# Post-norm block of low-rank attention and a top-2 mixture of experts: shorter score stacks, earlier loads of x, and an expert stage that begins while the last batches' tail is still open

## The chip, the cores and the metric

One core of one Trainium2 chip runs the whole program in one launch. The metric is device time in microseconds (us), the median of several executions. The engines are named as in the profile: PE is TensorE (matmuls), DVE is VectorE, ACT is ScalarE, POOL is GpSimd and SP is SyncE, which here only waits and issues DMAs.

## The reference

The input x is 16 batches of 512 tokens of 128 channels. Cut to what matters:

```python
q, k, v = heads(x @ Wq.T + bq), heads(x @ Wk.T + bk), heads(x @ Wv.T + bv)      # 16 heads of 8
zq, zk, zv = q @ V, k @ V, v @ V                                                # V, U: 8 x 8
att = softmax(einsum('bhqr,bhkr->bhqk', zq, zk) / sqrt(8))
y = einsum('bhqk,bhkr->bhqr', att, zv) @ U.T
x = layernorm(x + merge(y) @ Wo.T + bo)
p, i = top_k(softmax(x @ gate_w.T), 2); p = p / sum(p)
h = relu(einsum('td,ehd->teh', x, w1) + b1)                                     # 8 experts, 512 hidden
out = einsum('ted,te->td', einsum('teh,edh->ted', h, w2) + b2, combine(p, i))
return layernorm(x + out)
```

Only the two chosen experts of a token count, so the kernel routes each of the 8192 tokens to two experts instead of computing all eight.

## The kernel before

There are three stages, one behind the other, with a barrier between them.

**Setup** (L227 to L367). The weights are folded, and SP fills rows of the score stacks in device memory that never change: 16 stores of blank rows and rows of ones (`blank`, `k_ones`, L241 to L248), whose landing SP waits for (`blanks_stored`) ahead of a store of blank token rows (`routed_d<-pad_rows`, L252), which it waits for too. The first attention work can't begin before this block has ended on every engine.

**Attention** (L408 to L968). The function `schedule` (L408) unrolls bodies n = -2 to 17 with 32 steps each. The body of batch n holds its own scores, and besides: the projections of batch n+2 (transposition of x, L457; q and k, L465 and L488), v of batch n+1, the row maxima of the next scores, which run 24 steps ahead (LAG), and what follows the attention of n-1 and n-2: normalisation, output projection (L480), layernorm, gate (L526), choice of the two experts, ranks (L494, L497), and the scatter of token rows to their experts' areas in device memory (`routed_d`, POOL, L855, 8 indirect DMAs per batch). So the bodies of n = 16 and 17 hold no scores, only that tail.

- q and k are each split in three bf16 parts. The products of parts are made by one matmul: a *stack* of rows holds them one below the other, 8 positions of 8 ranks, 64 rows, for each of two heads. Six positions are pairs of parts, one (`MAX_POS`) holds the three parts of the row maximum against rows of ones, one is blank. Maxima (`maxima`, matmul in L583; DVE reduces them, L808) and scores (`scores`, matmul in L565; ACT takes the exponential, L694) both run over all 64 rows.
- SP stores the parts of a batch (L920), waits for them, and loads the stacks by head group (L925, per group one DMA of 256 KB for k and one for q), then the first half of the max rows (L913, 6 small DMAs), then the third group; in the next body the fourth. x of batch n+2 (L930) is loaded at the start of body n. All of this is one in-order queue.
- PE's order of work is written out by hand: at step s the score matmuls of s, the maxima of s+24, every other step the four products with v (`av`, L546), and `misc(s)`, a piece of other work.

**Experts** (L1018 to L1240). 136 tiles of 128 routed tokens. Per tile: SP reads the tile's row from a table and loads 128 rows (L1039), PE transposes (L1057), multiplies with W1 (L1066) and, two tiles later, with W2 (L1074); ACT copies the expert's weights three tiles ahead (L1109) and applies the relu (L1117); DVE copies the transposition out (L1140 to L1142), adds biases (L1163, L1147) and combines (L1151); POOL halves x (L1200) and scatters the result rows (L1205). The table (DVE, `table` steps, L820 to L838) is made when the last batch has been routed. `loop_tiles` (L1018) unrolls 8 tiles, loops, and unrolls the last 8. The final layernorm over 16 batches follows (L1101, L1178 to L1227).

## Time and profile before

| | us |
|---|---|
| median of 3 runs | 1254.78 (1251.57 to 1260.56) |
| the profiled execution | 1257.83 |
| its span, first to last recorded instruction | 1255.7 |
| PE busy | 1064.8 (85% of the span) |
| DVE busy | 972.6 (77%) |
| ACT busy | 904.7 (72%) |
| POOL busy | 588.2 (47%) |

The profile is of one execution: each instruction with start and duration. "Busy" is the time in which an engine executed anything. A duration in a row that says x6 covers six instructions. What stands in square brackets behind a row is how long the engine had been idle and what released it. PEclk is the share of TensorE's full clock that was granted.

### The profile page before, as it was taken

Reading aid. Unit: us, or ns where it says so; the run is one execution under the profiler, and the core shown is the slowest. Engines: PE = TensorE matmul, PEld = TensorE weight load, DVE = VectorE, ACT = ScalarE, POOL = GpSimd, SP = SyncE. Lnnn points to the kernel's source line nnn. Section 1 sums busy time; section 2 is a strip of 40 time slices with the busy share of each in tenths; the row PEclk is TensorE's granted clock in tenths of the full one; section 3 lists DMA queues with packets and bytes.
Section 4 is the critical chain, followed back from the end, with each engine's and each line's share of the span. In section 5 each row is a group of like instructions: output and inputs, shape, how many; then the busy total and the mean of one; then the engine's idle time right before and its main releaser. Section 6 shows DMA issues by size and latency. Waiting matters only on the chain. (4 is left out here: it accounts for less than half of the span.)

```text
span 1255.7 us, 24651 instructions
## 1 busy us (share of the span) xinstructions
PE 1064.8 (85%) x7711; PEld 515.8 (41%) x7711; DVE 972.6 (77%) x2115; ACT 904.7 (72%) x1177; POOL 588.2 (47%) x827
## 2 busy tenths in 40 slices
PE   3378899889898888999989899888728999999967
PEld 2132222222222222222222222222218999999952
DVE  2378889789888898887988779698246888888845
ACT  1047788677787777867778677687718999999937
POOL 1123145272452634527245171521354777777745
PEclk9989999899999999988999889899958999999989
DMA  2932241332523315233252332410012222222246
GB/s 68 282 117 58 80 135 43 111 102 59 148 56 99 108 52 148 65 90 103 57 148 57 97 103 56 121 34 15 18 49 64 70 68 69 69 69 70 67 154 263
DMA packets 108789, 114.31 MB, mean 91 GB/s; under 512 B 19816, under 2 KB 82066, under 8 KB 108704
## 3 DMA queue, kind: packets, MB, share of 16 engines
q1 hardware_dynamic: 99104, 92.10, 25.8%
q0 software_dynamic: 8448, 16.93, 4.3%
q10 hardware_dynamic: 1152, 4.19, 0.8%
q8 instruction: 47, 0.77, 0.3%
q14 instruction: 38, 0.31, 0.1%
HBM read 64.45 MB, written 48.44 MB: 90 GB/s over the span
## 5 line engine op out<-in xcount | busy, mean ns | idle before, releaser
L808 DVE TENSOR_REDUCE row_max<-score_ps 128x2 f32<-128x1024 f32 x512 | 617.9, 1220 | 134.6 <-PE score_ps L583 94.0
L694 ACT ACTIVATE probs<-score_ps 128x1024 f32<-128x1024 f32 x512 | 521.7, 1023 | 150.8 <-PE score_ps L565 130.3
L546 PE MATMUL av_ps<-probs,v_one 128*9 128x512 f32 x2048 | 277.8, 615 | 8.2 <-ACT probs L694 6.4
L583 PE MATMUL score_ps<-k_stack,q_stack 64*128 64x512 bf16 x1024 | 204.0, 396 | 74.6 <-ACT probs L694 55.6
L565 PE MATMUL score_ps<-q_stack,k_stack 64*128 64x512 bf16 x1024 | 204.0, 396 | 24.2 <-DVE row_max L808 19.0
L389 POOL TENSOR_TENSOR max_parts<-neg_max,zeros 32x128 bf16<-32x128 f32 x32 | 14.3, 446 | 386.9 <-ACT neg_max L635 386.9
L1109 ACT ACTIVATE w_cur<-experts 128x1156 f32 x136 | 158.5, 1167 | 36.5 <-PEq L425 17.2
L565 PEld LDWEIGHTS score_ps<-q_stack,k_stack 64*128 64x128 bf16 x1024 | 49.2, 93 | 315.1 <-issue 156.6
L1205 POOL DMA_INDIRECT y_d<-y_out,place x136 | 136.8, 1006 | 43.4 <-issue 43.4
L855 POOL DMA_INDIRECT routed_d<-rows,slot_i x128 | 125.4, 980 | 62.2 <-issue 36.6
L1066 PE MATMUL up_ps<-xt_sb,w_cur 128*128 128x128 f32 x1088 | 145.6, 277 | 0.0
L1074 PE MATMUL down_ps<-w_cur,hidden_r 128*128 128x128 f32 x1088 | 143.4, 275 | 0.0
L1066 PEld LDWEIGHTS up_ps<-xt_sb,w_cur 128*128 128x128 f32 x1088 | 134.1, 194 | 0.0
L1074 PEld LDWEIGHTS down_ps<-w_cur,hidden_r 128*128 128x128 f32 x1088 | 132.3, 192 | 0.0
L583 PEld LDWEIGHTS score_ps<-k_stack,q_stack 64*128 64x128 bf16 x1024 | 51.5, 95 | 131.6 <-ACT probs L694 87.8
L1163 DVE TENSOR_TENSOR hidden<-up_ps,w_cur 128x512 f32<-128x512 f32 x136 | 93.7, 689 | 3.6 <-PE up_ps L1066 3.2
L1117 ACT ACTIVATE hidden_r<-hidden 128x512 f32<-128x512 f32 x136 | 85.2, 626 | 6.7 <-DVE hidden L1163 5.2
L1200 POOL TENSOR_TENSOR half_x<-x_rows_sb,halves 128x128 f32<-128x128 f32 x136 | 53.4, 393 | 35.8 <-DVE y_out L1151 26.2
L546 PEld LDWEIGHTS av_ps<-probs,v_one 128*9 128x9 f32 x2048 | 30.6, 88 | 89.9 <-issue 84.5
L1147 DVE TENSOR_TENSOR y_bias<-down_ps,w_cur 128x128 f32<-128x128 f32 x136 | 39.6, 291 | 28.9 <-issue 26.0
L623 ACT ACTIVATE y_sb<-av_ps 128x512 f32<-128x512 f32 x64 | 38.2, 598 | 29.0 <-remote 16.6
L1057 PE MATMUL xt_ps<-ident,x_rows_sb 128*128 128x128 f32 x136 | 37.8, 278 | 18.0 <-DMA x_rows_sb<-routed_d 18.0
(189 smaller groups left out, 1144.5 us busy)
## 6 DMA issues: line engine op xcount, KB each, us to landing
k_stack<-k_stack_d SPq DMA_DIRECT2D x64, 256.0 KB, 3.6
q_stack<-q_stack_d SPq DMA_DIRECT2D x64, 256.0 KB, 4.2
x_rows_sb<-routed_d SPq DMA_DIRECT2D x136, 65.0 KB
q_stack_d<-q_parts SPq DMA_DIRECT2D x32, 192.0 KB
...
```

Source lines behind the costliest of these rows:

```text
L546: last = nc.tensor.matmul(av_ps[32 * g:32 * g + V_COLS, :], v_one[n.parity][:, kb, HG * hg + g, :], probs[:, (2 * j + g // 2) % P_RING, g ...
L565: last = nc.tensor.matmul(exp_bank(b, s)[:, a, :], k_stack[b.parity][at, c, kb * P:(kb + 1) * P], q_stack[b.parity][at, c, :], start=True, ...
L583: last = nc.tensor.matmul(max_bank(b, s)[:, a, :], q_stack[n.parity][at, c, g * P:(g + 1) * P], k_stack[n.parity][at, c, :], start=True, s ...
L694: nc.scalar.activation(probs[:, s % P_RING, :, :], exp_bank(b, s)[:, :, :], ACT.Exp).then_inc(S["exp_done"], 1)
L808: nc.vector.tensor_reduce(row_max[:, m // (STEPS // 2), :, m % (STEPS // 2)], max_bank(b, s)[:, :, :], AX.X, ALU.max).then_inc(S["red_done ...
L855: nc.gpsimd.indirect_dma_start(routed_d, bass.IndirectOffsetOnAxis(ap=slot_i[n.parity][:, w, t:t + 1], axis=0), rows[n.parity][:, w, t, :] ...
L1066: last = nc.tensor.matmul(up_ps[u % 4][:, h * P:(h + 1) * P], w_cur[u][:, h * P:(h + 1) * P], xt_sb[u % 2][:, :], start=True, stop=True)
L1074: last = nc.tensor.matmul(down_ps[u % 2][:, :], hidden_r[u % 4][:, h, :], w_cur[u][:, HID + h * D:HID + (h + 1) * D], start=(h == 0), stop ...
L1109: nc.scalar.activation(w_cur[u][:, :], experts[:, bass.ds(e, 1), :].rearrange("p a h -> p (a h)"), ACT.Copy).then_inc(M["w_copied"], 1)
L1117: nc.scalar.activation(hidden_r[u % 4][:, :, :], hidden[u % 4][:, :, :], ACT.Relu).then_inc(M["relu_out"], 1)
L1163: nc.vector.tensor_tensor(hidden[u % 4][:, :, :], up_ps[u % 4][:, :].rearrange("p (h t) -> p h t", t=P), w_cur[u][:, B1].unsqueeze(2).to_b ...
L1205: nc.gpsimd.indirect_dma_start(y_d, bass.IndirectOffsetOnAxis(ap=place[u][:, :], axis=0), y_out[u][:, :], None, bounds_check=2 * B * T - 1 ...
```

## The change

Three things are done.

1. The stacks get 6 positions of 8 ranks: maxima run over 48 rows, scores over 51, the three last being the parts of the row maximum. The rows of ones in k's stack are set once in SBUF, by two DVE memsets of 128 x 4096 bf16 at the start. The 16 stores of blank rows go, with the wait for them; the blank token rows are still stored, not waited for in setup. A stack is loaded by two DMAs of 96 KB instead of one of 256 KB, one for each half of the partitions. The k parts of the first batch are stored from ACT's queue.
2. x is loaded one body sooner: in the body of n SP loads batch n+3 (as soon as x of n+1 has been transposed), where it loaded n+2.
3. `schedule` ends with the body of batch 15. The experts begin with 32 full tiles (`FIRST`) filled by tokens of batches 0 to 13, by a table of their own (`first_tiles`, 18 small DVE operations in the body of batch 15). Their rows are loaded by SP, 12 tiles ahead of the block's end, 20 behind it, into a buffer of 32 tiles. The tail of batches 14 and 15 is cut into pieces, and `attention(j)` writes the pieces behind (on PE: ahead of) the work of tile j on each engine. At tile 31 SP stores the pads, waits for the table of the rest and for all scatters, and loads tile 32. All tiles use one PSUM buffer for the transposition, where there were two.

```diff
-POS = 8
-MAX_POS = 5
-MAX_ROW = MAX_POS * R
-ROWS = POS * R
+POS = 6
+ROWS = 64
+SCORE_ROWS = POS * R
+MAX_ROWS = 3
...
+FIRST = 32
+FIRST_GROUP = 4
+FIRST_EARLY = 12
...
-                    sp.wait_ge(bo_loaded, 16)
-                    sp.wait_ge(blanks_ready, 4)
-                    for n in range(2):
-                        for stack_d, row, tile in ((q_stack_d[n], MAX_POS, blank), (q_stack_d[n], POS - 1, blank),
-                                                   (k_stack_d[n], MAX_POS, k_ones), (k_stack_d[n], POS - 1, blank)):
-                            for a in range(2):
-                                sp.dma_start(stack_d[a, row, :, :, :].rearrange("r c t -> (r c) t"),
-                                             tile[a * ROWS:(a + 1) * ROWS, :]).then_inc(blanks_stored, 16)
-                    sp.wait_ge(blanks_stored, 16 * 16)
...
-                    sp.wait_ge(pads_stored, 16)
...
+                    for n in range(2):
+                        nc.vector.memset(k_stack[n][:, :, :], 1.0).then_inc(ones_ready, 1)
...
-                for n in range(-2, B + 2):
+                for n in range(-2, B):
...
-                                at = slice(a * ROWS, (a + 1) * ROWS)
+                                at = slice(a * ROWS, a * ROWS + SCORE_ROWS + MAX_ROWS)
...
-                        if proj and not is_first(b) and not is_first(p1):
...
+                            n3 = n1 + 2
...
+                            sp.dma_start(x_in[n3.parity][:, :, :], tokens(x_rows, n3)).then_inc(x_loaded[n3.parity], 16)
...
+                        if proj and not is_first(b):
...
+                            if t < FIRST - 1:
+                                return
+                            for loaded in first_loaded:
+                                sp.wait_ge(loaded, 16 * FIRST_GROUP)
+                            store_pads()
+                            sp.wait_ge(rest_table, REST_STEPS)
+                            sp.wait_ge(pads_stored, 16 + 16 * E)
+                            for n in range(2):
+                                sp.wait_ge(scattered[n], B // 2 * 8 * 16)
+                            return
...
+                        if j == 0:
+                            pe.wait_ge(S["yn_sb"], n15.count(HG, 3))
+                            y_transpose(pe, n15, 3)
+                        elif j == 1:
+                            pe.wait_ge(S["yn_sb"], n15.count(HG, 4))
+                            y_to_rows(pe, n15)
+                        elif j == 2:
+                            pe.wait_ge(S["ynt_sb"], n15.count(1, 1))
+                            project_out(pe, n15)
+                        elif j == 4:
+                            pe.wait_ge(S["res_ready"], n15.count(1, 1))
+                            pe.wait_ge(S["top_step"], n14.count(TOP_STEPS, 13))
+                            rank(pe, n14)
+                        elif j == 6:
+                            pe.wait_ge(S["slot_step"], n14.count(SLOT_STEPS, 2))
+                            pe.wait_ge(S["x1_ready"], n15.count(QT, QT))
+                            x1_to_rows(pe, n15)
+                        elif j == 7:
+                            pe.wait_ge(S["x1t_sb"], n15.count(1, 1))
+                            gate(pe, n15)
+                        elif j == 13:
+                            pe.wait_ge(S["logits_sb"], n15.count(1, 1))
+                            pe.wait_ge(S["top_step"], n15.count(TOP_STEPS, 13))
+                            rank(pe, n15)
...
-                        nc.tensor.transpose(xt_ps[u % 2][:, :], x_rows_sb[u][:, 0:D], ident[:, :]).then_inc(M["xt_done"], 1)
...
+                        nc.tensor.transpose(xt_ps[:, :], x_tile(i, u)[:, 0:D], ident[:, :]).then_inc(M["xt_done"], 1)
...
+                        if j == 3:
+                            deviation(pool, n15)
+                        elif j == 9:
+                            places(pool, n15)
+                        elif 11 <= j <= 18:
+                            if j == 11:
+                                rows_ready(pool, n14)
+                                for loaded in first_loaded:
+                                    pool.wait_ge(loaded, 16 * FIRST_GROUP)
+                            scatter(pool, n14, j - 11, j - 10)
+                        elif 19 <= j <= 26:
+                            if j == 19:
+                                rows_ready(pool, n15)
+                            scatter(pool, n15, j - 19, j - 18)
...
+                            for t in range(halved_by(tile_index(i, u) - 1), halved_by(tile_index(i, u))):
+                                halve(*divmod(t, RING), i * RING + u)
...
+                        return max(j + 2, min(2 * j + 4, 24)) if j >= 0 else 0
```

SP's queue in the middle of a batch's body, before. From top to bottom: the k parts are stored, two head groups of stacks loaded, the first half of the max rows, the third group, then x and, in the next body, the fourth group.

```order
L920 DMA k_stack_d<-k_parts 64x2x512 x2
L920 DMA k_stack_d<-k_parts 64x512 x2
L925 DMA k_stack<-k_stack_d 128x1024
L925 DMA q_stack<-q_stack_d 128x1024
L925 DMA k_stack<-k_stack_d 128x1024
L925 DMA q_stack<-q_stack_d 128x1024
L913 DMA q_stack<-max_parts 1x16x128 x6
L925 DMA k_stack<-k_stack_d 128x1024
L925 DMA q_stack<-q_stack_d 128x1024
L930 DMA x_in<-L_attn_x 128x4x128
```

And after the change:

```order
L410 DMA k_stack_d<-k_parts 64x2x512 x2
L410 DMA k_stack_d<-k_parts 64x512 x2
L1039 DMA k_stack<-k_stack_d 48x1024 x2
L1039 DMA q_stack<-q_stack_d 48x1024 x2
L1039 DMA k_stack<-k_stack_d 48x1024 x2
L1039 DMA q_stack<-q_stack_d 48x1024 x2
L1032 DMA q_stack<-max_parts 1x16x128 x6
L1039 DMA k_stack<-k_stack_d 48x1024 x2
L1039 DMA q_stack<-q_stack_d 48x1024 x2
L1045 DMA x_in<-L_attn_x 128x4x128
```

Nothing has changed places; each stack load has become two, so eight issues instead of four stand ahead of the max rows. The load of x stands in its old place and is of the batch behind.

PE between the last attention work and the first tile, before: the tail of batch 15 (output transposition, output projection, transposition for the gate, gate, then its ranks), and only then, behind the block's end, tiles.

```order
L470 MATMUL misc_ps<-ident,y_norm 128x128 x4
L480 MATMUL misc_ps<-wo_t,y_t 128x128 x4
L517 MATMUL misc_ps<-ident,rows 128x128 x4
L526 MATMUL misc_ps<-gate_t,x_t 128x8 x4
L497 MATMUL misc_ps<-chosen_any,before 128x8
```

After, from the block's end on; L415 is the last y transposition, L530 and L536 are the lines that were L470 and L480, and L1246, L1255 and L1263 are the tile's transposition, W1 and W2 products.

```order
L1246 MATMUL xt_ps<-ident,first_rows 128x128
L415 MATMUL misc_ps<-ident,y_sb 128x128 x4
L1246 MATMUL xt_ps<-ident,first_rows 128x128
L1255 MATMUL up_ps<-xt_sb,w_cur 128x128 x4
L530 MATMUL misc_ps<-ident,y_norm 128x128 x4
L1246 MATMUL xt_ps<-ident,first_rows 128x128
L1255 MATMUL up_ps<-xt_sb,w_cur 128x128 x4
L536 MATMUL misc_ps<-wo_t,y_t 128x128 x4
L1246 MATMUL xt_ps<-ident,first_rows 128x128
L1255 MATMUL up_ps<-xt_sb,w_cur 128x128 x4
L1263 MATMUL down_ps<-w_cur,hidden_r 128x128 x4
```

The tail's pieces now stand one per tile, in PE's order, with the tiles' matmuls in between.

POOL at the end of the attention, before: the last batch's scatters (L855) are one block, and the tiles' operations follow behind the block's end.

```order
L855 DMA routed_d<-rows,slot_i 66688x130 x6
L861 IOTA rows 128x8
L855 DMA routed_d<-rows,slot_i 66688x130 x8
L425 UNCONDITIONAL_BRANCH
L1195 UNCONDITIONAL_BRANCH
L1200 TENSOR_TENSOR half_x<-x_rows_sb,halves 128x128 x3
L1205 DMA y_d<-y_out,place 16384x128
```

After; L523 is the scatter of token rows to their experts, L1470 the halving, L1475 the scatter of a tile's result.

```order
L593 IOTA rows 128x8
L1470 TENSOR_TENSOR first_half<-first_rows,halves 128x128 x2
L1475 DMA y_d<-y_out,place 16384x128 x2
L523 DMA routed_d<-rows,slot_i 66688x130
L1475 DMA y_d<-y_out,place 16384x128
L523 DMA routed_d<-rows,slot_i 66688x130
L1475 DMA y_d<-y_out,place 16384x128
L523 DMA routed_d<-rows,slot_i 66688x130
```

The 16 scatters of batches 14 and 15 stand in tiles 11 to 26, each behind the scatter of that tile's predecessor.

## Rows read from the trace of the kernel before

**Rows 1.** Windows by stage: stretch, length, busy us (instructions) by engine, PEclk, DMA share, GB/s

```profile
0.00:21.90 21.90, 5.73 (x23) 4.97 (x24) 2.45 (x13) 2.59 (x9) 6.09 (x51) 1.00 0.36 91
21.90:82.50 60.60, 32.04 (x137) 14.92 (x137) 33.37 (x32) 13.14 (x24) 11.40 (x12) 0.93 0.60 183
82.50:908.00 825.50, 727.81 (x5111) 218.04 (x5111) 679.94 (x1056) 624.96 (x797) 343.39 (x439) 0.96 0.30 84
908.00:946.20 38.20, 7.86 (x64) 5.64 (x64) 15.11 (x54) 6.08 (x14) 17.82 (x21) 0.58 0.14 44
946.20:1006.50 60.30, 59.53 (x512) 59.24 (x513) 49.07 (x183) 54.64 (x63) 39.02 (x58) 0.95 0.26 70
1006.50:1210.00 203.50, 200.98 (x1802) 200.77 (x1800) 172.31 (x634) 179.28 (x209) 150.30 (x215) 1.00 0.24 65
1210.00:1255.70 45.70, 30.90 (x64) 12.23 (x64) 20.36 (x144) 24.05 (x64) 20.18 (x33) 0.85 0.72 276
```

**Rows 2.** Timeline of the start: start us, us, engine, line, what, count [idle, releaser]

```profile
5.67 0.17 DVE L333 COPY vu_rep<-misc_ps 128x16 f32<-128x16 f32 x1 [5.67 <-PE misc_ps L305]
9.72 0.48 DVE L352 MEMSET av_ps<- 128x512 f32 x1
13.16 0.29 DVE L355 TENSOR_TENSOR bo_b<-misc_ps,bo_b 128x128 f32<-128x128 f32 x1 [2.95 <-PE misc_ps L328]
...
19.63 0.37 SPq L252 DMA_DIRECT2D routed_d<-pad_rows  x1
...
21.91 1.08 PE L457 MATMUL misc_ps<-ident,x_in 128*128 128x128 f32 x4 [8.79 <-PEq L227]
...
33.42 3.86 SPq L920 DMA_DIRECT2D k_stack_d<-k_parts  x6
```

**Rows 3.** Waits of PE over the whole span: total us, times, longest

```profile
PE misc_ps L457 <- DMA x_in<-L_attn_x: 9.7, 8, 2.3
...
PE score_ps L565 <- DMA q_stack<-max_parts: 4.0, 2, 3.5
```

**Rows 4.** Timeline of one batch's body, SP's queue and PE

```profile
429.73 0.33 SPq L925 DMA_DIRECT2D k_stack<-k_stack_d  x1
...
431.05 0.44 SPq L925 DMA_DIRECT2D q_stack<-q_stack_d  x1
432.76 4.66 SPq L913 DMA_DIRECT2D q_stack<-max_parts  x6
...
439.74 0.39 PE L565 MATMUL score_ps<-q_stack,k_stack 64*128 64x512 bf16 x2 [1.33 <-DVE row_max L808]
...
443.70 0.66 PE L457 MATMUL misc_ps<-ident,x_in 128*128 128x128 f32 x4 [1.84 <-DMA x_in<-L_attn_x]
```

**Rows 5.** Timeline from the last exponential to the first tiles, by engine

```profile
909.17 0.60 ACT L623 ACTIVATE y_sb<-av_ps 128x512 f32<-128x512 f32 x1 [1.17 <-PE av_ps L546]
...
913.70 1.58 PE L480 MATMUL misc_ps<-wo_t,y_t 128*128 128x128 f32 x8 [0.78 <-ACT y_t L654]
921.36 1.11 PE L517 MATMUL misc_ps<-ident,rows 128*128 128x128 f32 x4 [6.08 <-ACT rows L629]
...
928.44 0.17 PE L497 MATMUL misc_ps<-chosen_any,before 128*128 128x8 bf16 x1 [3.34 <-DVE chosen L746]
...
946.24 0.47 PE L1057 MATMUL xt_ps<-ident,x_rows_sb 128*128 128x128 f32 x1 [17.29 <-DMA x_rows_sb<-routed_d]
...
940.47 0.96 POOL L855 DMA_INDIRECT routed_d<-rows,slot_i  x1 [0.31 <-issue]
```

**Rows 6.** Groups by line, 1006.5 to 1200 us: busy, mean ns, idle before

```profile
L1205 POOL DMA_INDIRECT y_d<-y_out,place x103 | 103.6, 1006 | 33.1 <-issue 33.1
...
L1200 POOL TENSOR_TENSOR half_x<-x_rows_sb,halves 128x128 f32<-128x128 f32 x102 | 40.1, 393 | 17.9 <-DVE y_out L1151 15.7 <-issue 0.5
```

**Rows 7.** Windows of 2 us behind the first scores, columns as in rows 1

```profile
88.00:90.00 2.00, 2.00 (x13) 0.25 (x12) 0.90 (x1) 1.57 (x2) 0.00 (x0) 0.50 0.14 40
...
92.00:94.00 2.00, 1.47 (x14) 0.33 (x14) 2.00 (x2) 1.40 (x2) 0.00 (x0) 1.00 0.00 0
```

777 lines of the change are left out of this document (479 added, 298 removed).

## The prediction

> **What bounds the kernel now.** I read the windows by stage first [rows 1]. Attention proper, 82.5 to 908, is 825.5 us with PE 727.8 busy, DVE 679.9, ACT 625.0: three engines each over 75%, a tight ring. Then come two stretches in which TensorE does little: the start (21.9 us, PE 5.7 busy) and the hand-over from attention to experts (908 to 946.2: 38.2 us, PE 7.9 busy). Experts from 1006.5 on are PE-bound (201.0 of 203.5). So gains are looked for in the start, in waits inside the ring, and in the 38.2 us; the timelines of the start and the hand-over [rows 2, 5] and PE's waits for x [rows 3] say what ends there last.
>
> **A, the start.** PE's first attention work, L457, begins at 21.91 after 8.79 us of idleness that the block's end closes [rows 2]. DVE's last setup operation is over at 13.16+0.29 = 13.45; what keeps the block open is SP's 16 stores, their landing, and the pads store at 19.63 with its own (to about 21.5, by the start of L457). Without these the block ends when DVE does. DVE gets two memsets: a 128x512 memset took 0.48 us, so 4096 elements take 8 x 0.485 = 3.9 and both 7.8. They stand ahead of an operation that before began at 5.67, and if DVE takes them up within the first us it is free at about 8.6; the small copies behind are partly waits for PE, which shrink. I put the delay of L355 at 1.1 us over the 13.45 (0 if the queue behind is all slack, 8.6-5.67 = 2.9 if none is) and 0.4 for the barrier: L457 at 15.0, 6.9 sooner. Then 21.9 to 82.5 [rows 1]: six k stores at 3.86 us go to ACT's queue and run beside the q stores (-1), stack loads become twice as many (+0.9: four issues more ahead of the first maxima at 0.47), and the expert weights' load, which follows on SP's queue and isn't moved by the change, gives back some 0.7 (a tenth of the 6.9, an estimate). A = -6.9 -1 +0.9 +0.7 = **-6.3** (bounds -8 to -4).
>
> VectorE could have been faster at bf16 than at the fp32 of the row. The Trainium skill ("VectorE: DVE Perf Modes", section "Zero memsets can be issued as uint32 (trn2)") says that a memset takes one cycle per element whatever the dtype, and that only zeros have a wider form; these are ones. By a halved price A would be at most 1.1 better; no row of before shows a bf16 memset on DVE.
>
> **B, x sooner.** PE waited for x 8 times, 9.7 us in all [rows 3]; one is at 443.70, 1.84 us, where x had been issued a few us before and landed too late [rows 4]. A body earlier it has some 50 us, so all but the first waits go. I take -8, not -9.7, since a wait that goes may open the next one: scores wait for DVE's reduction in the same steps (bounds -10 to +3). Against it stands SP's queue: four more issues ahead of the max rows. One issue takes 0.43 plus its gap, 0.47; from the first to the last of the group's four before, 429.73 to 431.05+0.44 = 431.5 [rows 4]. Eight instead of four end 1.9 us later, but SP waited from 431.5 to 432.76 for the split of the maxima, so the max rows start at about 433.4 instead of 432.76, 0.7 later. The last of them is issued at 432.76+4.66 = 437.4, and the scores that need them begin at 439.74, released by DVE's reduction and not by them; with a landing of 1 to 1.5 us, an estimate that keeps below the 2.3 between the two, the slack is 0.8 to 1.3. PE waited for them only twice in all, 3.5 of the 4.0 us once [rows 3]. Cost 0; without that cover it is rival 4. Shorter stacks alone move nothing on PE: the matmul's columns stay 512, and its duration is what the ring sees. I price fewer rows and 25% less bytes at 0 (bounds 0 to -3).
>
> **C, the hand-over.** Before, the chain of the last batch runs: y copied out by ACT 909.17+0.60, output projection 913.70, x1 for the gate 921.36 (after 6.08 us for the layernorm), choice of experts to 928.44 (3.34 idle), 16 scatters of which the last is 940.47+0.96, and, behind SP's row load, the first tile's transposition 946.24 [rows 5]. After, the first tile needs none of it: T0 = 909.77 plus a barrier of 0.4 = 910.2. That is 36.0 us sooner. What is given back:
>
> - Tiles 0 to 7. Their own matmuls are 8 x 1.9 = 15.2, less two W2 products of the first two tiles (1.8), plus the tail's matmuls, some 4.2 (the output projection 1.58 and the transposition 1.11 in rows 5, at a low clock, the other four less). PE's order is fixed, so a piece that isn't ready holds the tiles behind it. I estimate the chain's waits, as they come to PE, at 1.4 (normalised y), 2.6 (its copy), 3.3 (choice of 14: the 3.34 of rows 5), 5.3 (x1 ready: 6.08 before), 1.1 = 13.7; the copy is dearer than before because DVE and ACT do a tile's work between. Plus some 2 us in which weights and relu of the first tiles aren't there. Sum: tile 8 begins at T0+34.
> - Tiles 8 to 12 carry three choice operations each on DVE; its busy time per tile is 172.3 us/107 tiles = 1.61 [rows 1], and three small operations with their waits for one another add 0.66: 2.27 per tile. Step 11 of POOL, which runs behind the result of tile 10, starts at T0+34+3x2.27+3 tiles of lag = T0+45.5 to 50; I take 47.
> - POOL then has a tile's scatter (1.006 + 0.31 issue gap [rows 6]) and a token scatter of the same kind (0.96 + 0.30) in each step: 2 x 1.28 = 2.57, so 12 steps are 30.9, and the last four (23 to 26) also a halving of 0.39: 4 x 2.96 = 11.8. Sum 42.7. POOL is then the slowest engine of these steps, above PE's 1.9. Last token scatter out at T0+47+42.7 = T0+90.
> - From it to tile 32: landing, SP's row load, its landing. Before this was 941.43 to 946.24 = 4.8 with the barrier; I take 3.8. The pads' 8 stores and the table (DVE tiles 15 to 22) are done by then.
>
> So tile 32's transposition comes at T0+94 = 1004.2. Before it came at 1006.5 [rows 1]: C = **-2.3**. The bounds: -19 (scatter chain from T0+45 and POOL not behind at all in steps 11 to 18) to +9 (chain to T0+55, half clock in tiles 0 to 7). It is an odd result: 36 us sooner at the start, and 34 given back, because 16 scatters that cost 1.26 each before cost 2.57 to 2.96 each in turns with those of the tiles; but the 32 tiles then lie under them.
>
> **D, behind tile 32.** 104 tiles remain at PE's pace as before, 1006.5 to 1210 [rows 1]; the 102 halvings of rows 6 in 193.5 us show 1.90 per tile. One PSUM buffer for the transposition makes PE wait for DVE's copy before the next one, with a whole tile's products in between: 0 (to +3 if the copy is late behind DVE's other work of the tile). The final layernorm is unchanged. D = 0.
>
> Sum: -6.3 -8 -2.3 = **-16.6**. Against the profiled execution (1257.83) that is 1241.2. The profiled one is 3 us above the median of the three runs, so the median forecast is 1254.8 - 16.6 = 1238.
>
> **The rivals.**
>
> *1. The tiles hide the scatters.* If the chain is short (POOL's step 11 at T0+40) and the halvings ahead let POOL run behind without stopping PE, tile 32 comes when PE has done 32 tiles: some 31.5 us for the first eight (the chain shorter by 2.5), 24 at 1.9 = 45.5, so T0+77. C = -19.3: 1238 - 17 = 1221. For: PE alone needs no more. Against: POOL's own sum from step 11 is 42.7, whatever PE does.
>
> *2. The hand-over loses.* TensorE ran at a mean 0.58 of its clock from 908 to 946 [rows 1]; between the pieces of a waiting chain it idles again. If tiles 0 to 7 run at half clock (+4) and each chain link on DVE, ACT and POOL waits for the tile's operation ahead of it (+4), C is +6: 1247.
>
> *3. The clock stays at half through tiles 14 to 31.* PE is then some 70% busy (1.9 of 2.6). At half clock a tile takes 3.8 instead of 2.6; 18 tiles, +21.7 beyond the forecast: 1260 or so. In 92 to 94, with 1.47 of 2 us busy, the granted clock was 1.00 (2.4 GHz), after 0.50 (1.2 GHz) in a fully busy window at 88 [rows 7], so it holds at 73% busy there, which speaks against it. The Trainium skill ("TensorE: Matmul & The Clock Gate", section "HAM oscillation — how this bites in real kernels") tells of a kernel whose short bursts between waits each began cold; rows 7 show such a cold start and its end, and no second fall at 73% busy. By that rule the time would be the 1260 just given.
>
> *4. The other side: SP's queue comes late.* Eight stack issues in a body instead of four. If the max rows' slack were the smaller one read, 0.8, and the landing of twice as many DMAs takes 2 us more than before, scores wait some 1.9 us in each of 16 batches: +30, minus the rest of the forecast: 1238 + 30 = 1268. It decides from about 0.9 us per batch, where the -16.6 is eaten up. For: the queue is in order and carries 12 stack, 6 max and 12 store DMAs before x. Against: DMA share is 0.30 over the stage [rows 1] and bytes fall by a quarter.
>
> *5. The change doesn't do what it says* only for B: if the waits for x ended on another late piece (PE's own step order), they'd move, not go. That is in B's upper bound.
>
> **How the numbers follow.** Forecast 0.53, rival 1 0.17, rival 2 0.15, rival 3 0.06, rival 4 0.09. The range 1221 to 1254 takes in the forecast, rivals 1 and 2 and the bounds of A and B (4 and 11 us to the slow side). About 1% (12.5 us) is what a measurement of this kernel can tell from no change. Faster by over 1% is below 1242: rival 1 and four fifths of the forecast's weight, 0.6. Slower by over 1% is above 1267: rival 4, 0.09. Within: the rest, 0.31.
>
> **What would show each step.** A: L457's successor starts near 15.0 and the two memsets last 3.9 each. B: the wait of PE for x is below 2 us in all, no wait for `max_parts` beyond the two of before. C: the first expert transposition stands at T0 = 1 us behind the last y copy; the waits of PE in tiles 0 to 7 sum to about 14; POOL is busy or in its issue gap without a hole from step 11 to step 26, each step 2.6 to 3.0; tile 32 is released by a row load behind the last token scatter. D: 1.90 per tile behind it. Wrong would be: tile 32 at T0+80 or less (rival 1), above T0+100 (rival 2), a granted clock of 0.5 after tile 14 (3), PE waiting for `max_parts` or `k_stack` in most batches (4).

## The result, and the profile after

| us | before | after |
|---|---|---|
| median (range, executions) | 1256.57 (1251.57 to 1260.56, 4) | 1278.24 (1275.49 to 1281.41, 4) |
| profiled execution | 1257.83 | 1276.26 |
| its span | 1255.7 | 1274.5 |

The ratio is 1.018 with a 95% interval of 1.0136 to 1.0222: slower by over 1%, where 1238 and "faster" were forecast. The time lies 24 us beyond the upper end of the range, too. Executions of one kernel differ with the mean granted clock (nine of one experiment ran from 1241.9 at 0.960 to 1267.6 at 0.927), so medians below are over all executions of a kernel, ratios leave out those over 1.5% above its fastest one, and a term below 5 us isn't read from either but from the stages of a trace.

The stages of after, columns as in [rows 1]: the start, to the first scores, attention, tiles 0 to 7 with the tail's pieces, tiles 8 to 31, the rest of the tiles, the final layernorm.

```profile
0.00:15.60 15.60, 6.09 (x23) 5.02 (x23) 9.18 (x17) 2.59 (x9) 4.13 (x47) 1.00 0.24 60
15.60:76.00 60.40, 32.08 (x137) 14.78 (x137) 33.37 (x32) 13.15 (x24) 11.40 (x12) 0.99 0.59 175
76.00:910.00 834.00, 746.13 (x5119) 221.65 (x5119) 677.18 (x1067) 623.90 (x797) 344.04 (x439) 0.94 0.27 75
910.00:947.70 37.70, 23.76 (x147) 22.29 (x147) 15.23 (x67) 19.36 (x26) 11.29 (x23) 0.73 0.17 44
947.70:1018.00 70.30, 54.11 (x425) 52.04 (x425) 47.43 (x181) 42.68 (x52) 46.38 (x58) 0.89 0.15 47
1018.00:1223.00 205.00, 203.48 (x1800) 203.29 (x1800) 171.99 (x631) 177.57 (x207) 148.52 (x212) 0.99 0.24 66
1223.00:1274.50 51.50, 30.80 (x64) 12.20 (x64) 20.36 (x144) 24.12 (x64) 20.90 (x34) 0.82 0.63 245
```

Against [rows 1] with its borders put at the same events, the span's +18.8 us is made of:

| stage | before | after | difference | forecast |
|---|---|---|---|---|
| start to the first scores | 82.6 | 76.0 | -6.5 | -6.3 |
| first scores to the last `av` product | 826.5 | 834.0 | +7.5 | -8 |
| from there to tile 32's transposition | 97.4 | 108.0 | +10.6 | -2.3 |
| tile 32 to tile 135, transpositions | 195.3 | 197.9 | +2.5 | 0 |
| ACT's last output to the span's end | 2.6 | 7.5 | +5 | 0 |

The start, where [rows 2] stood:

```profile
1.71 3.47 DVE L327 MEMSET k_stack<- 128x4096 bf16 x1 [1.71 <-PEq L1518]
5.98 3.47 DVE L327 MEMSET k_stack<- 128x4096 bf16 x1 [0.80 <-issue]
...
15.02 0.29 DVE L353 TENSOR_TENSOR bo_b<-misc_ps,bo_b 128x128 f32<-128x128 f32 x1 [3.49 <-PE misc_ps L322]
```

```profile
15.63 1.09 PE L747 MATMUL misc_ps<-ident,x_in 128*128 128x128 f32 x4 [0.65 <-PEq L238]
```

The block ends when DVE does, at 15.31 instead of 21.9. PE's waits in attention, of after, where [rows 3] stood:

```profile
PE score_ps L838 <- ACT probs L933: 59.1, 73, 2.9
...
PE score_ps L820 <- DMA q_stack<-max_parts: 5.9, 3, 3.7
```

No wait for x is left, of 9.7 us before, and those for the max rows are two or three short ones. Yet attention is 7.5 us longer. PE's own work has grown: 728.8 us busy from 82 to 909 before, 746.1 from 76 to 910 now, at a mean granted clock of 0.96 and 0.94. Where the time went is plain in the groups by line (busy, mean ns, idle before), here the products of `probs` with v in before:

```profile
L546 PE MATMUL av_ps<-probs,v_one 128*9 128x512 f32 x2048 | 277.8, 615 | 8.2 <-ACT probs L694 6.4 <-issue 1.8
```

and of after:

```profile
L426 PE MATMUL av_ps<-probs,v_one 128*9 128x512 f32 x2048 | 285.9, 632 | 8.0 <-ACT probs L933 8.0
```

They are 8.1 us dearer with the same count and shape, and the change doesn't touch them. So it is the clock. By the granted clock of these traces, added up from the first scores to the last `av` product, TensorE ran at half of it (1.2 GHz) for 63.7 us of attention before and for 100.8 after; half clock below is always this sum. (The recorded expectations use narrower counts, such as 54.6 and 85.3 for these two and 11.8 for `paced_scatter`.) Most of these stretches stand behind a stall that both kernels have once in each of the bodies 2 to 13. Here it is in before:

```profile
640.31 0.60 ACT L623 ACTIVATE y_sb<-av_ps 128x512 f32<-128x512 f32 x1 [1.36 <-remote]
...
641.07 1.23 DVE L808 TENSOR_REDUCE row_max<-score_ps 128x2 f32<-128x1024 f32 x1 [2.25 <-remote]
...
642.11 0.39 PE L583 MATMUL score_ps<-k_stack,q_stack 64*128 64x512 bf16 x2 [2.50 <-ACT probs L694]
```

and in after:

```profile
634.93 0.96 POOL L523 DMA_INDIRECT routed_d<-rows,slot_i  x1 [0.30 <-issue]
...
636.89 0.60 ACT L434 ACTIVATE y_sb<-av_ps 128x512 f32<-128x512 f32 x1 [1.92 <-remote]
636.98 1.23 DVE L973 TENSOR_REDUCE row_max<-score_ps 128x2 f32<-128x1024 f32 x1 [2.13 <-remote]
...
638.46 0.61 PE L838 MATMUL score_ps<-k_stack,q_stack 48*128 48x512 bf16 x2 [2.82 <-ACT probs L933]
...
639.00 1.89 PE L426 MATMUL av_ps<-probs,v_one 128*9 128x512 f32 x8
```

DVE and ACT stand still at once, released by something that the trace can't name ("remote"), at the end of a row of POOL's scatters, and PE stands 2.4 to 3.1 us in the twelve. Behind the two shown the score pair took 0.39 us before and 0.61 after, eight `av` products 1.05 (642.43) and 1.89. In before the clock fell at 6 of the 12 stalls, in after at 11. A batch behind a fall of 10.2 us takes about 54 us, one with 3.4 us or none 51 to 52.

One trace of each can't carry that comparison, though. `unrolled`, described below, has the attention of before line for line; in its profiled execution (1261.21, the slowest of eight) the clock fell at 11 of the 12 stalls too, with 87.1 us of half clock and 829.6 of attention. Four traces with both new parts (after, `no_handover`, `scatter_sooner`, `scatters_last`) have 832.8 to 835.2. What tells the kernels apart is the times of all their executions and the mean granted clock of each over the whole program, given with the experiments.

The hand-over, where [rows 5] stood. PE of after:

```profile
910.97 0.45 PE L1246 MATMUL xt_ps<-ident,first_rows 128*128 128x128 f32 x1 [0.97 <-PEq L715]
...
947.71 0.31 PE L1246 MATMUL xt_ps<-ident,first_rows 128*128 128x128 f32 x1
...
975.70 0.47 PE L1246 MATMUL xt_ps<-ident,first_rows 128*128 128x128 f32 x1 [3.00 <-DVE xt_sb L1390]
975.97 1.91 PE L1255 MATMUL up_ps<-xt_sb,w_cur 128*128 128x128 f32 x8
...
987.17 0.47 PE L1246 MATMUL xt_ps<-ident,first_rows 128*128 128x128 f32 x1 [4.01 <-DVE xt_sb L1390]
...
1005.11 0.33 PE L1246 MATMUL xt_ps<-ident,first_rows 128*128 128x128 f32 x1 [3.01 <-DVE xt_sb L1390]
...
1017.99 0.45 PE L1246 MATMUL xt_ps<-ident,x_rows_sb 128*128 128x128 f32 x1 [3.45 <-DMA x_rows_sb<-routed_d]
```

Tile 0 starts at T0 = 910.97, tile 8 at 947.71 (T0+36.7). Tiles 19, 22 and 28 wait 3 to 4 us, and what holds DVE there reads as in attention:

```profile
973.57 0.69 DVE L1411 TENSOR_TENSOR hidden<-up_ps,w_cur 128x512 f32<-128x512 f32 x1 [3.04 <-remote]
...
984.40 0.69 DVE L1411 TENSOR_TENSOR hidden<-up_ps,w_cur 128x512 f32<-128x512 f32 x1 [3.72 <-remote]
```

POOL's chain of token scatters (L523), with those of the tiles (L1475) in turn:

```profile
962.17 0.98 POOL L1475 DMA_INDIRECT y_d<-y_out,place  x1 [1.24 <-DVE y_out L1399]
963.46 0.97 POOL L523 DMA_INDIRECT routed_d<-rows,slot_i  x1 [0.30 <-issue]
...
975.82 0.98 POOL L1475 DMA_INDIRECT y_d<-y_out,place  x1 [2.71 <-DVE y_out L1399]
...
986.45 1.20 POOL L1475 DMA_INDIRECT y_d<-y_out,place  x1 [3.26 <-DVE y_out L1399]
...
1012.47 0.97 POOL L523 DMA_INDIRECT routed_d<-rows,slot_i  x1 [0.30 <-issue]
```

The chain begins at T0+51.2, takes 51.3 us to 1013.44, and tile 32 follows 4.55 later, at T0+107.0.

### The profile page after: what moved, and what is told of

It is laid out like the page before. It is cut to its first block and busy times, and to the rows that moved or that the text cites. A ratio compares the mean times of both kernels' runs of the same rounds, so it can differ in the third digit from the quotient of the medians.

```text
span 1274.5 us, 24572 instructions
## 1 busy us (share of the span) xinstructions
PE 1096.5 (86%) x7711; PEld 531.3 (42%) x7711; DVE 974.7 (76%) x2139; ACT 903.4 (71%) x1177; POOL 586.7 (46%) x823
## 5 line engine op out<-in xcount | busy, mean ns | idle before, releaser
L426 PE MATMUL av_ps<-probs,v_one 128*9 128x512 f32 x2048 | 285.9, 632 | 8.0 <-ACT probs L933 8.0
L838 PE MATMUL score_ps<-k_stack,q_stack 48*128 48x512 bf16 x1024 | 208.4, 404 | 76.6 <-ACT probs L933 59.1
L820 PE MATMUL score_ps<-q_stack,k_stack 51*128 51x512 bf16 x1024 | 206.2, 400 | 21.2 <-DVE row_max L973 14.2
L820 PEld LDWEIGHTS score_ps<-q_stack,k_stack 51*128 51x128 bf16 x1024 | 49.3, 93 | 320.2 <-issue 154.4
L1475 POOL DMA_INDIRECT y_d<-y_out,place x136 | 137.1, 1008 | 81.3 <-DVE y_out L1399 42.8
L1255 PE MATMUL up_ps<-xt_sb,w_cur 128*128 128x128 f32 x1088 | 152.5, 286 | 0.6 <-ACT w_cur L1319 0.6
L1263 PE MATMUL down_ps<-w_cur,hidden_r 128*128 128x128 f32 x1088 | 147.5, 280 | 0.0
L523 POOL DMA_INDIRECT routed_d<-rows,slot_i x128 | 125.1, 978 | 37.4 <-issue 34.7
L1255 PEld LDWEIGHTS up_ps<-xt_sb,w_cur 128*128 128x128 f32 x1088 | 141.8, 203 | 1.0 <-DVE xt_sb L1390 1.0
L1263 PEld LDWEIGHTS down_ps<-w_cur,hidden_r 128*128 128x128 f32 x1088 | 136.6, 197 | 0.0
L1411 DVE TENSOR_TENSOR hidden<-up_ps,w_cur 128x512 f32<-128x512 f32 x136 | 93.6, 688 | 20.7 <-PE up_ps L1255 13.6
L838 PEld LDWEIGHTS score_ps<-k_stack,q_stack 48*128 48x128 bf16 x1024 | 51.7, 95 | 134.9 <-ACT probs L933 87.1
L426 PEld LDWEIGHTS av_ps<-probs,v_one 128*9 128x9 f32 x2048 | 30.6, 89 | 91.1 <-issue 83.2
L1395 DVE TENSOR_TENSOR y_bias<-down_ps,w_cur 128x128 f32<-128x128 f32 x136 | 39.4, 290 | 32.0 <-issue 19.8
L1470 POOL TENSOR_TENSOR half_x<-x_rows_sb,halves 128x128 f32<-128x128 f32 x104 | 40.8, 392 | 19.3 <-DVE y_out L1399 17.4
L415 PE MATMUL misc_ps<-ident,y_sb 128*128 128x128 f32 x256 | 45.1, 302 | 0.0
```

What stands on the lines that cost most here:

```text
L426: last = nc.tensor.matmul(av_ps[32 * g:32 * g + V_COLS, :], v_one[n.parity][:, kb, HG * hg + g, :], probs[:, (2 * j + g // 2) % P_RING, g ...
L523: nc.gpsimd.indirect_dma_start(routed_d, bass.IndirectOffsetOnAxis(ap=slot_i[n.parity][:, w, t:t + 1], axis=0), rows[n.parity][:, w, t, :] ...
L820: last = nc.tensor.matmul(exp_bank(b, s)[:, a, :], k_stack[b.parity][at, c, kb * P:(kb + 1) * P], q_stack[b.parity][at, c, :], start=True, ...
L838: last = nc.tensor.matmul(max_bank(b, s)[:, a, :], q_stack[n.parity][at, c, g * P:(g + 1) * P], k_stack[n.parity][at, c, :], start=True, s ...
L1255: last = nc.tensor.matmul(up_ps[u % 4][:, h * P:(h + 1) * P], w_cur[u][:, h * P:(h + 1) * P], xt_sb[u % 2][:, :], start=True, stop=True)
L1263: last = nc.tensor.matmul(down_ps[u % 2][:, :], hidden_r[u % 4][:, h, :], w_cur[u][:, HID + h * D:HID + (h + 1) * D], start=(h == 0), stop ...
```

## The experiments

Fifteen kernels ran, each beside the kernel before on the same chip; not all of them on one chip. "Plus" and "minus" are medians against the before beside it. Diffs are against before unless said.

### Which part costs

`x_only` has part 2 alone, `stacks_only` part 1 alone, `no_handover` both without part 3.

```diff
-                        if proj and not is_first(b) and not is_first(p1):
-                            wait(sp, S["xt_done"], b.count(1, 1))
-                            sp.dma_start(x_in[n2.parity][:, :, :], tokens(x_rows, n2)).then_inc(x_loaded[n2.parity], 16)
+                        if nxt and n1.c + 2 < B:
+                            n3 = n1 + 2
+                            sp.wait_ge(S["xt_done"], n1.count(1, 1))
```

> The kernel before with the loads of x one body sooner, and nothing else of the change. Theory P (the pace of the batches): the waits for x (9.7 us in 8 places) are gone, but the stall of 2.5 to 2.9 us that stands in each body from 2 to 13 stays and now meets the clock so that it falls to half more often (54.6 us of half clock between the first and last scores before, 85.3 us after the whole change); then attention takes as long as before or longer, 825 to 835 us, and the time is 1255 to 1265. Rival Q (the stacks do it): without the new stacks the gain of x stays, attention is 816 to 819 us and the time 1246 to 1249.

> The kernel before with stacks of 48 and 51 rows, two loads of 96 KB for each of 256 KB, the ones set in SBUF and no stores of blank rows. Theory P: the start is 6 us shorter, attention as before within what the clock gives (820 to 832), x is still waited for; the time 1245 to 1256. Rival Q: attention takes 8 to 15 us longer than before, from the doubled issues on SP's queue or from the matmuls of 48 rows; the time is 1258 to 1264, and PE waits for stacks or max rows in most bodies.

> Stacks and x together, on the kernel before, experts as before. By the trace of the changed kernel this has a start 6 us shorter, and attention 7 us longer; hand-over, tiles and end as before: 1256 to 1259. If the hand-over costs what the trace of the changed kernel says (10.5 us from last product with v to tile 32, 2.5 us of low clock behind it, 5 us at the program's end), this kernel is 18 us faster than the changed one. Rival: the hand-over disturbs the attention too, then this one is below 1250.

Measured: x sooner 1249.5 (10 executions), minus 6.9, ratio 0.993 (0.9898 to 0.9961). Stacks alone 1267.5 (5), plus 11.1, ratio 1.0086 (1.0053 to 1.0118), although PE's first attention work begins at 15.63 there too, 6.3 sooner than before. Both 1263.0 (9), plus 6.7; its two quickest executions (1241.9 and 1250.2) alone give 0.991 (0.9866 to 0.9957), the other seven, 1261.1 to 1267.6, lie above all 18 of before. The whole change is plus 21.7. So by medians the hand-over costs 15, the stacks 11, and x gives back 4 to 7. By the stages above the hand-over costs 18 (10.6, 2.5 and 5), and 19 in the pair with spread scatters below, whose executions lie closer together. Part 2 does about what it was priced at; the other two don't.

The clock goes with the times: four of the five executions with the new stacks alone had a mean of 0.932 to 0.937 (the profiled one, 1256.0, had 0.952), the 18 of before 0.940 to 0.956. Of the expectations, rival Q of `x_only` came true (attention 817.5). `stacks_only` is beyond rival Q's 1264, and PE waited for max rows only 3 times there (5.5 us), not in most bodies. `no_handover` by its median is above both of its ranges.

### The stall: whose is it

In mid-body of before stand four scatters in a row, then the split of the maxima, then two more; two stand at the body's start. `early_scatter` moves the four to the two at the start:

```diff
-                            scatter(p2, 0, 2)
+                            scatter(p2, 0, 6)
...
-                        if prev2:
-                            scatter(p2, 2, 6)
```

> The kernel before, but POOL issues six of a batch's eight scatters at the body's start instead of two there and four behind the splits of k. Theory S: the stall at step 25 of bodies 2 to 13, in which DVE and ACT start 2 us after what they waited for had ended, comes from scatters in flight together with the stores of the k parts (both are there in exactly these 12 bodies); moved away, the stall goes or shrinks and the clock does not fall: attention 780 to 800 us, time 1215 to 1235. Rival: it comes from the stores alone or from something else of the bodies' form; then the 12 stalls stay at 2.2 us on DVE and the time is 1252 to 1262.

Measured 1287.0 (4), plus 30.6, ratio 1.0243 (1.021 to 1.0276), beyond both expectations. There are twelve stalls of 1.8 to 3.1 us on DVE, and all stand behind the moved scatters, none in mid-body: the stall went along with them. They don't explain the loss: DVE's "remote" waits sum to 29.8 us there and to 26.8 in before, while attention is 18 us longer and the way from it to tile 32 is 5 longer; that stays open. POOL, DVE and ACT at the start of a body, by the timeline:

```profile
314.48 0.97 POOL L855 DMA_INDIRECT routed_d<-rows,slot_i  x1 [0.30 <-issue]
...
316.99 1.23 DVE L808 TENSOR_REDUCE row_max<-score_ps 128x2 f32<-128x1024 f32 x1 [2.51 <-remote]
...
316.95 1.02 ACT L694 ACTIVATE probs<-score_ps 128x1024 f32<-128x1024 f32 x1 [3.63 <-remote]
```

SP issued nothing from 311.42 (the last of the small max rows) to beyond 320 there, and from 310 to 318 the DMA share is 0.10 to 0.21, so it isn't the transfers of stacks that hold DVE and ACT. `paced_scatter` keeps the eight scatters but never lets more than two follow at once: two at the body's start as before, two behind the split of the maxima, at steps 30 and 32, four in the next body, at steps 2, 4, 6 and 8.

```diff
+                        if 3 <= b.c <= B:
+                            for k in range(4, 8):
+                                if cur:
+                                    pool.wait_ge(S["st_done"], b.count(STEPS, 2 * k - 6))
+                                scatter(b + -3, k, k + 1)
...
+                        if prev2 and cur:
+                            for k in (2, 3):
+                                pool.wait_ge(S["st_done"], b.count(STEPS, 26 + 2 * k))
+                                scatter(p2, k, k + 1)
```

> The kernel before, but six of a batch's eight scatters are spread: two behind the split of the maxima at steps 30 and 32, four in the next body at steps 2, 4, 6 and 8, where POOL stood idle. Theory S2 (four or more scatters one behind the other hold up the other engines' semaphores for 2 us; with six in a row the stall moved to those six): the 12 stalls of 2.2 us on DVE go, with the half clock behind them; attention 780 to 800 us, time 1215 to 1235. Rival: the stall is of the k stores or of step 25; it stays at 12 times 2.2 us and the time is 1250 to 1262.

```profile
433.60 1.03 POOL L855 DMA_INDIRECT routed_d<-rows,slot_i  x1 [2.93 <-PE score_ps L565]
436.40 0.96 POOL L855 DMA_INDIRECT routed_d<-rows,slot_i  x1 [1.77 <-PE score_ps L565]
```

```profile
L808 DVE TENSOR_REDUCE row_max<-score_ps 128x2 f32<-128x1024 f32 x488 | 590.6, 1221 | 72.6 <-PE score_ps L583 71.0
```

Measured 1236.9 (4), minus 20, ratio 0.984 (0.98 to 0.988). "Remote" is gone from the row of the reduction (26.8 us of its waits in before), there is no such stall in any body, half clock in attention is 19.8 us, and a batch takes 50 us; the time is 2 us above theory S2's range. Same scatters, same cost on POOL: spreading them takes the stall away.

A row of four alone doesn't bring it on, however. The trace of before has a thirteenth row of four, in body 14, 1.27 us apart as well, with nothing standing still; these are its last scatter and DVE behind it:

```profile
843.05 0.96 POOL L855 DMA_INDIRECT routed_d<-rows,slot_i  x1 [0.30 <-issue]
843.63 1.23 DVE L808 TENSOR_REDUCE row_max<-score_ps 128x2 f32<-128x1024 f32 x1 [0.16 <-PE score_ps L583]
```

That body splits and stores no parts of q and k: the DMA share is 0.10 from 841 to 843, where it is 0.81 and 0.89 in 636 to 638 and 638 to 640, beside the row that ends in the stall at 641.07. In the tail of before eight scatters in a row (930.97 to 941.43) ran beside DVE's table operations, none of which waits (they depend on no other engine). With rows of six the stall comes without stores (the lines of `early_scatter` above). So a row of scatters is one condition, and stores in flight, or a longer row, look like a second; no run separates them.

### The stacks: rows or issues

`short_matmul` lets the matmuls of before run over 48 and 51 rows, out of stacks that are loaded whole, by 256 KB DMAs; `double_issue` splits each of these loads in two and keeps 64 rows.

```diff
-MAX_POS = 5
+MAX_POS = 6
...
-                                at = slice(a * ROWS, (a + 1) * ROWS)
+                                at = slice(a * ROWS, a * ROWS + MAX_ROW + 3)
```

```diff
+                                for a in range(2):
+                                    sp.dma_start(stack[n.parity][a * ROWS:(a + 1) * ROWS, pairs, :],
```

> The kernel before with the same stacks of 64 rows, the same loads and stores, but the three max rows moved to rows 48 to 50, so that the maxima run over 48 rows and the scores over 51. Theory K (fewer rows of the array in use bring the clock down more often): half clock inside the attention rises from 51 to 56 us to 80 to 97, attention from 817 to 827 us to 830 to 836, and the time to 1262 to 1270. Theory P (the rhythm alone): nothing is changed that any engine sees, so the time stays 1252 to 1261.

> The kernel before with each stack load of 256 KB split in two of 128 KB; all else, the rows of the matmuls too, as before. Theory Q2 (SP's eight issues ahead of the max rows): PE waits for stacks or max rows more often, or the later max rows shift the rhythm; attention 832 to 840 and 1262 to 1270. Theory K: 1252 to 1261, as before.

The first edit also puts the parts of q and k in another order in the stack, which no run separates from the number of rows.

Measured: `short_matmul` 1270.4 (4), plus 13.6, ratio 1.0106 (1.0064 to 1.0147), attention 831.6, at the edge of theory K's range. All four executions lie above all seven of before, at a mean clock of 0.930 to 0.941 against 0.942 to 0.955. (Its trace has 95.5 us of half clock, which by itself says little beside the 87.1 of `unrolled`.) `double_issue` 1299.2 (4), plus 42.4, ratio 1.034, far beyond theory Q2's 1270. PE's waits of the latter:

```profile
PE misc_ps L457 <- DMA x_in<-L_attn_x: 36.0, 14, 3.7
...
PE score_ps L565 <- DMA q_stack<-max_parts: 21.9, 9, 5.3
```

In before these two are 9.7 and 4.0 us, so the larger loss is at x, which stands behind the stacks in the queue. The queue's late end is real, and dearer here than in the change: by the median, an issue of 64 rows took 0.60 us (1.24 for two with the gap), one of 48 rows 0.42 (0.89 for two, in after) and the whole one of 128 rows 0.43:

```profile
408.72 1.24 SPq L926 DMA_DIRECT2D q_stack<-q_stack_d  x2
```

Both edits lose. But in `short_matmul` the stalls are there too, so fewer rows may matter only behind a stall. `paced_short` is `paced_scatter` with the edit of `short_matmul`.

> The kernel before with the spread scatters and the matmuls of 48 and 51 rows on stacks of 64 (loads as before). Theory K1 (fewer rows bring the clock down, stall or no stall): half clock in the attention 30 us or more, where the spread scatters alone have 11.8, and 1243 to 1250 against 1237. Theory K2 (they only do so behind a stall of 2 us and more): 1234 to 1240 and under 20 us of half clock.

Measured 1245.1 (4), ratio 0.989 (0.9862 to 0.9922), against 0.984 of `paced_scatter`. Windows over attention, first of `paced_scatter`, then of `paced_short`:

```profile
83.00:884.00 801.00, 711.28 (x5119) 212.37 (x5119) 697.13 (x1056) 624.82 (x797) 340.17 (x435) 0.99 0.30 86
```

```profile
83.00:897.00 814.00, 727.30 (x5119) 214.47 (x5119) 698.07 (x1056) 624.48 (x797) 339.09 (x435) 0.96 0.30 85
```

With no "remote" stall in either, the same matmuls over fewer rows have half clock for 60.3 us instead of 19.8, and PE is 16 us busier. The traces exaggerate, being of the slowest execution of one and the quickest of the other; but all four of `paced_short` had a mean clock of 0.949 to 0.955 and all four of `paced_scatter` 0.958 to 0.964. The medians differ by 8 us, the ratios to before by 0.5% or 6 (the two ran on different chips). So theory K1 holds: the edit of the rows costs clock without a stall. Beside the stalls it cost 13.6.

### The hand-over

`scatter_sooner` (against after) puts the scatters of batch 14 in tiles 7 to 14 and those of 15 in tiles 16 to 23.

```diff
-                        elif 11 <= j <= 18:
+                        elif 16 <= j <= 23:
...
+                        if 7 <= j <= 14:
```

> The changed kernel, but the scatters of batch 14 stand in tiles 7 to 14 instead of 11 to 18, those of 15 in tiles 16 to 23 instead of 19 to 26. If the chain of POOL from tile 11 on sets when tile 32 comes (108 us behind the last product with v), it comes 5 to 8 us sooner: time 1270 to 1273. Rival: the stalls of 3 to 4 us that PE has at tiles 18, 21 and 27 come from scatters following each other without a pause; their number stays at 3 or rises to 5, and tile 32 comes no more than 3 us sooner (1275 to 1281). The 5 us at the program's end stay under both if they are of the longer unrolled program.

Measured 1281.0 (4), plus 24.2, ratio 1.0194: as after, and the rival's range. Last `av` product to tile 32 is 104.5 instead of 108.0, with four stalls of 1.7 to 2.6 instead of three of 3 to 4. Starting earlier bought 3.5 us; the stalls stayed. `scatters_last` (against after) takes all 16 out of the tiles' turns and puts them in one block at tile 29; `unrolled` (against before) writes 40 tiles out in place of 8, to see whether the code itself costs.

```diff
+                        elif j == 29:
+                            rows_ready(pool, n14)
+                            rows_ready(pool, n15)
+                            scatter(pool, n14, 0, 8)
+                            scatter(pool, n15, 0, 8)
```

```diff
-                with engine.Fori(1, TILES // RING - 1) as i:
+                for i in range(5):
+                    for u in range(RING):
+                        step(i, u)
+                with engine.Fori(5, TILES // RING - 1) as i:
```

> The changed kernel, but none of the 16 scatters of batches 14 and 15 stands between tiles; all 16 follow in one block at tile 29. If the alternation of two scatters per tile causes the stalls of PE at tiles 18, 21 and 27 (3 to 4 us each), tiles 8 to 29 run without them, tile 29's transposition comes at 42 to 46 us behind tile 8's (1.9 to 2.1 per tile) instead of 58, and the block of 16 (16 x 1.28 = 20.5 us) lies bare: tile 32 comes 104 to 110 us behind the last product with v, as now. If the stalls have another cause, they are at the same tiles and tile 32 comes 118 us or more behind it. If the 5 us at the end come from where the scatters stand, the end is 2.5 us here.

> The kernel before with five times eight tiles written out ahead of the loop, as the changed kernel has them, and nothing else. The changed kernel ended 5 us later behind its last operation (7.5 us from ACT's last output to the end, 2.6 before). If that is the longer program, this kernel shows 7 to 8 us there and 1259 to 1264; if it comes from what the hand-over does, 2.5 us and 1252 to 1261.

Measured: `scatters_last` 1284.2 (2), plus 25.7. From tile 8 to 29 PE now needs 45.6 us, where after needed 60.0; first of `scatters_last`, then of after:

```profile
948.36 0.31 PE L1246 MATMUL xt_ps<-ident,first_rows 128*128 128x128 f32 x1
...
994.01 0.27 PE L1246 MATMUL xt_ps<-ident,first_rows 128*128 128x128 f32 x1
```

```profile
1007.73 0.42 PE L1246 MATMUL xt_ps<-ident,first_rows 128*128 128x128 f32 x1
```

So without two scatters per tile these 21 tiles are 14 us shorter, 10 of it the three stalls, and no "remote" wait is left on DVE there; the block then costs more than that, as PE waits 26.9 us for it at tile 32. That is 116.1 in all, where 104 to 110 was expected: POOL runs behind PE and begins the block at 1002.66, 8.7 us behind tile 29's transposition. `unrolled` 1254.2 (8), ratio 0.999 (0.9951 to 1.0028): written-out tiles cost nothing, at the end of the program neither (2.5 us there).

### Everything with spread scatters

`paced_attention` is before with parts 1 and 2 and the spread scatters, `paced_x` before with part 2 and these, `paced_after` after with these in bodies 2 to 14 (the tail as it was), and `paced_x_start` is `paced_x` with the wait for the blank rows moved out of setup:

```diff
-                    sp.wait_ge(blanks_stored, 16 * 16)
-                    sp.wait_ge(pads_stored, 16)
...
+                            if is_first(b):
+                                sp.wait_ge(blanks_stored, 16 * 16)
```

> The kernel before with the new stacks, x sooner and the spread scatters, experts as before. Theory S2 (the stall is made by scatters in a row) with theory K (fewer rows only matter where a stall lets the clock fall): without stalls the stacks' loss of 13 us goes, the gains of the start (6) and of x (7) stay on top of the 20 of the spread scatters: 1222 to 1230. Rival: short stacks cost clock by themselves, stall or no stall: half clock of 50 us or more in the attention and 1238 to 1250.

> The kernel before with x sooner and the spread scatters, stacks of 64 rows and setup as before. If x's waits (11.0 us in the kernel with spread scatters alone) are gains in full, 1226 to 1230; if DVE and ACT set the pace once the stalls are gone, 1232 to 1237.

> The changed kernel with the spread scatters in bodies 2 to 14 (in body 15 they stay where the change has them). If stacks, x and hand-over add up with the spread scatters as the parts measured so far, this is the version above plus 15 us of hand-over: 1237 to 1247. If the hand-over lost only because the attention's clock was low behind it, it is below the version with the old hand-over.

> The kernel before with x sooner, the spread scatters, and the wait for the blank rows moved from setup to where the first stacks are loaded (the stores stay). The start is 7 to 8 us shorter as in the changed kernel, and nothing else moves: 1215 to 1219. Rival: the earlier start runs into the expert weights' load or meets the clock worse, and 1220 to 1226 is measured.

| | median (n) | ratio (95%) | attention | half clock in it |
|---|---|---|---|---|
| `paced_x` | 1224.0 (4) | 0.971 (0.9652 to 0.976) | 791.4 | 8.3 |
| `paced_attention` | 1231.3 (4) | 0.976 (0.9707 to 0.9819) | 804.1 | 56.5 |
| `paced_after` | 1250.3 (10) | 0.996 (0.9921 to 1.0003) | | |
| `paced_x_start` | 1221.4 (4) | 0.971 (0.968 to 0.9738) | | |

`paced_attention` and `paced_x_start` miss the first of their ranges by a little, `paced_x` is 2 us under both of its, and `paced_after` is 3 above. The stacks still lose: 7.3 us by the medians, and 12.7 in attention by the traces, of which the start gives back 5.4. The mean clock was 0.947 to 0.956 with the new stacks and 0.969 to 0.973 without, in four executions each on one chip. Twice as many issues show in what PE waits for ahead of the scores. The max rows and DVE's reduction, in `paced_attention`:

```profile
PE score_ps L547 <- DMA q_stack<-max_parts: 26.4, 15, 4.0
...
PE score_ps L547 <- DVE row_max L790: 12.6, 24, 1.3
```

and in `paced_x`:

```profile
PE score_ps L565 <- DVE row_max L808: 38.9, 65, 1.4
...
PE score_ps L565 <- DMA q_stack<-max_parts: 5.0, 3, 3.5
```

The wait has moved rather than grown: both together are 39.0 us with the doubled issues and 43.9 without. And rows alone lengthened attention by 13 us in the traces of `paced_short` and `paced_scatter`, about as much as rows and doubled issues together do here. So a price of the doubled issues of 48 rows isn't shown.

The hand-over costs 19 us on top (1250.3 against 1231.3), about as in after. `paced_x_start` gets 3.6 us of the start without touching the stacks, not the 7 to 8 expected (PE begins at 19.06, in `paced_x` at 22.62). Its 1221.4 is the lowest median of this study, 35 to 37 us below before and 57 below after; its ratio to the before beside it is that of `paced_x`, which ran on another chip, so that it is faster than `paced_x` is shown by the start in the trace alone.

What stays open: the 5 us at the end. SP waits at the last barrier for PE's queue:

```profile
SPq L1170 <- PEq L1170: 5.2, 1, 5.2
```

and of before:

```profile
SPq L1032 <- PEq L1032: 0.2, 1, 0.2
```

From ACT's last output to the end of the span, all four kernels with the new hand-over have 7.3 to 7.8 us, all the others 2.5 to 2.7. It isn't the number of tiles written out (`unrolled`) nor where the scatters are (`scatters_last`). Nor is it shown what "remote" is; only what takes it away.

## Why the prediction was wrong

**A held**, with some luck. -6.3 forecast, -6.5 measured. The memsets took 3.47 us each, not 3.9: bf16 0.85 ns per element against 0.94 in the fp32 row, far from half. As to the dtype, that agrees with the Trainium skill ("VectorE: DVE Perf Modes", section "Zero memsets can be issued as uint32 (trn2)"), by which it makes no difference to a memset. They began at 1.71, which hid what this saved. L353 came at 15.02, PE's first work at 15.63 for 15.0; from there to the first scores it was 0.2 us less than before, where the terms came to 0.6 more. One of these terms was also worked out wrongly: four issues more at 0.47 are 1.9 us, not 0.9.

**B held in its mechanism.** The waits for x went, all of them, and `x_only` measured -6.9 for -8.

**The step that failed in B** is "Shorter stacks alone move nothing on PE: the matmul's columns stay 512, and its duration is what the ring sees. I price fewer rows and 25% less bytes at 0 (bounds 0 to -3)". The durations at a given clock are indeed the same, 0.39 us for a pair at full clock. But the clock isn't given. 48 and 51 rows instead of 64 cost 13.6 us in before (`short_matmul`) and 6 to 8 where nothing stalls (`paced_short`). The bounds left out a loss on no grounds but that the work was less. Why fewer rows are granted less clock is open.

**What wasn't read** is the stall itself. It was in the trace of before twelve times, 26.8 us as "remote" in the row of the reduction, and the same view as [rows 3] has a larger row that wasn't drawn on, PE's 55.6 us in 63 waits for `probs`, in which it hides. The forecast called attention "a tight ring" and took the ring's pace as fixed; with the scatters spread, the same ring runs 26 us shorter (800.7 against 826.5). But the change's loss in attention isn't theirs: the clock fell at 11 of them in after and at 6 in before, yet at 11 in `unrolled` too, and the stacks lose 12.7 us of attention where there is none (`paced_attention` against `paced_x`).

**C failed in the scatter chain.** T0 was 910.97 (forecast 910.2), tile 8 at T0+36.7 (T0+34), POOL's step 11 at T0+51.2 (T0+47), the chain 51.3 us (42.7), the rest to tile 32 4.6 (3.8): T0+107 for T0+94. The failed step is "12 steps are 30.9 ... 4 x 2.96 = 11.8. Sum 42.7", a sum of POOL's own times as if scatters cost others nothing. With two per tile, 1.28 us apart, PE stands 3 to 4 us three times behind DVE, whose own "remote" waits there are 3.0, 3.7 and 1.5, and POOL then waits in its turn for the tile's result (2.71 and 3.26 in the rows above); with the scatters out of the tiles these waits are gone (`scatters_last`). Rival 2 has the sign and, at T0+102, more than half the size, but not the place: it put its loss in tiles 0 to 7, which came 2.7 us late, where the chain took 8.6 more than forecast. (The terms for tiles 0 to 7 sum to 33.3, written as 34.)

**D** came out at +2.5 for 0: after the 3.45 us wait at tile 32 its eight W1 and eight W2 products took 1.92 and 1.91 us at half clock, for 1.06 each at full. The +5 at the end was not in any case.

**Rival 4's** mechanism, the late queue, is seen where an issue is dearer (`double_issue`), and as a wait that replaces another in `paced_attention`; in the change as run it is 5.9 us in after, for 4.0 before. It would have been the wrong reason for a right sign. **Rival 1** fell by `scatters_last` in part: PE alone does tiles 8 to 28 in 45.6 us, but the scatters have to be somewhere. **Rival 3**, a clock that stays at half through tiles 14 to 31, wasn't seen; between tile 14 and 31 it fell only behind stalls, as the 1.91 us row shows, for a few tiles each (13.7 us in all). The upper end of the range took 4 us from A, whose bound was 2.3 from its forecast; that changes nothing here.

Summed up over the medians: the start -6.3 as forecast, x -4.4 on top of the stacks for -8, the stacks in attention +17.4 (11.1 with the start's 6.3 put back) for 0, the hand-over with all that follows it +15 for -2.3 (and D's 0): +21.7 for -16.6.
